# Fused attention and feed-forward layer: the two rounds of values and the round of ones of a four-step cycle are issued in one block

## The reference, cut to what matters

```python
# x: (2, 1024, 1024) f32; 32 heads of 32 channels, 8 key/value heads (4 heads share one)
xn = layernorm(x)
q, k, v = bitnet_linear(xn, wq, sq), bitnet_linear(xn, wk, sk), bitnet_linear(xn, wv, sv)
scores = einsum('bhqd,bhkd->bhqk', q, k) / sqrt(32)
out = einsum('bhqk,bhkd->bhqd', softmax(scores), v)
x + bitnet_linear(out, wo, so) + ffn(xn)      # ffn: silu(xn @ gate) * (xn @ up) @ down, 4-bit weights
```

## Time and profile before

| | |
|---|---|
| median of 3 runs | 2541.43 us (2540.97 to 2541.54) |
| the profiled execution | 2542.98 us, of which the span of the trace is 2541.0 us |
| mean granted TensorE clock, profiled execution | 0.967 of full speed |
| attention with its cycles in steady order (372 to 1151 us) | PE busy 777.61 of 779.00 us, DVE 608.92, ACT 609.37, POOL 710.12 |
| rest of the attention, without row products (1151 to 1193 us) | PE busy 35.34 of 42.00 us, ACT 33.17 |

### The profile page before, as it was taken

One profiled execution on the slowest core, in us unless ns is written; L12 is line 12 of the kernel. 1 busy time (PEld: TensorE's weight loads), 2 busy tenths in 40 slices (PEclk: granted clock), 3 DMA queues, 4 the chain that ended last, 5 costly groups with the idle time before them and its releaser, 6 DMA issues.

```text
span 2541.0 us, 33630 instructions
## 1 busy us (share of the span) xinstructions
PE 2384.1 (94%) x12408; PEld 969.4 (38%) x12408; DVE 1826.3 (72%) x2362; ACT 1549.7 (61%) x1988; POOL 983.7 (39%) x545
## 2 busy tenths in 40 slices
PE   2399899999999999997699999999999999999998
PEld 1344323333333333332344444444444444444444
DVE  6756587777777777771646777777777777777777
ACT  3533347777777777776225666666665566666664
POOL 1000038989999999998000121121001111221000
PEclk9599979999999999998799999999999999999999
DMA  4100035555555555564221111112112311113111
GB/s 171 66 4 34 11 79 82 87 90 81 91 79 88 90 82 91 79 93 60 100 95 42 34 50 34 34 50 100 42 37 98 106 34 34 50 34 145 64 41 67
DMA packets 173710, 174.65 MB, mean 69 GB/s; under 512 B 87586, under 2 KB 119202, under 8 KB 173558
## 3 DMA queue, kind: packets, MB, share of 16 engines
q1 hardware_dynamic: 111286, 150.62, 18.9%
q0 software_dynamic: 62272, 22.03, 11.3%
HBM read 160.08 MB, written 65.45 MB: 89 GB/s over the span
## 4 chain that ended last, share of the span: by engine, by line
PE 90%; DVE 4%; DMA 1%; ACT 1%; issue 1%; SPq 1%; POOL 1%; DVEq 0%; ACTq 0%; POOLq 0%
PE ps L1309 30%; PE ps L1325 15%; PE ps L1212 10%; PE ps L1185 10%; PE ps L1201 8%; PE ps L1160 7%; PE ps L1224 4%; PE ps L1289 4%; DVE zone L934 1%; DVE zone L812 1%; POOL zone L504 1%; PE ps L1341 0%; DMA zone<-in_L_attn_o_weight_dram 0%; DVE zone L781 0%; DVE zone L782 0%
## 5 line engine op out<-in xcount | busy, mean ns | idle before, releaser
L1309 PE MATMUL ps<-xT,zone 128*128 128x512 f16 x3584 | 774.6, 379 | 3.6 <-DVE zone L1098 2.8
L934 DVE TENSOR_REDUCE zone<-ps 128x1 f32<-128x512 f32 x1024 | 637.5, 682 | 180.2 <-PE ps L1185 180.2
L657 ACT ACTIVATE zone<-ps,sm 128x512 f32<-128x512 f32 x1024 | 626.1, 690 | 183.1 <-PE ps L1201 181.3
L504 POOL TENSOR_TENSOR zone<-zone 128x1024 f32<-128x1024 f32 x256 | 633.4, 2582 | 114.4 <-PE ps L1224 73.3
L1075 DVE TENSOR_SCALAR ps<-ps,zone_c 128x1024 f32<-128x1024 f32 x392 | 506.8, 1293 | 161.2 <-PE ps L1309 159.2
L725 ACT ACTIVATE ps<-ps,zone_c 128x1024 f32<-128x1024 f32 x392 | 426.6, 1088 | 261.4 <-PE ps L1309 259.6
L1309 PEld LDWEIGHTS ps<-xT,zone 128*128 128x128 f16 x3584 | 350.2, 98 | 427.3 <-DVE zone L1098 4.2
L1185 PE MATMUL ps<-zone 96*128 96x512 f16 x1024 | 402.5, 395 | 11.2 <-DMA zone<-zone 10.5
L1201 PE MATMUL ps<-zone 98*128 98x512 f16 x1024 | 388.2, 382 | 4.0 <-ACT zone L657 4.0
L1325 PE MATMUL ps<-zone 128*128 128x512 f16 x1792 | 387.1, 379 | 0.0
L1086 DVE TENSOR_SCALAR ps<-ps,zone_c 128x1024 f32<-128x1024 f32 x216 | 279.2, 1293 | 93.1 <-PE ps L1325 92.9
(11 more groups left out here) (127 smaller groups left out, 1281.8 us busy)
## 6 DMA issues: line engine op xcount, KB each, us to landing
zone<-dequantised SPq DMA_DIRECT2D x84, 512.0 KB, 3.6
dequantised<-zero_points SPq DMA_DIRECT2D x84, 256.0 KB, 4.0
zone<-zone SPq DMA_DIRECT2D x384, 32.0 KB, 2.3
zone<-_attn_hidden_states_dram SPq DMA_DIRECT2D x16, 512.0 KB, 6.5
zone<-inverse_sums SPq DMA_DIRECT2D x128, 64.0 KB, 2.1
attention<-zone SPq DMA_DIRECT2D x32, 256.0 KB, 2.0
xT<-attention SPq DMA_DIRECT2D x4, 2048.0 KB, 13.2
dequantised<-in_L_ffn_gate_w_dram POOLq DMA_DIRECT2D x28, 256.0 KB, 6.2
```

The lines of the kernel that those rows point to most:

```text
L504: nc.gpsimd.tensor_tensor(duo[n % 3], prob[:, e % 8, :], prob[:, (e + 2) % 8, :], add).then_inc(s["sum_ok"], 1)
L657: A(prob[:, e % 8, m % 2 * 512:(m % 2 + 1) * 512], ps[:, 3 + m % 3, :], ACT.Exp, scale=gam[:, 0:1]).then_inc(s["exp_ok"], 1)
L934: V.tensor_reduce(mxs[:, u % 2, half, i % 16:i % 16 + 1], ps[:, (2 * i + half) % 3, :], AX, amax).then_inc(s["max_ok"], 1)
L1309: last = MM(ps[:, 4 * s2 + 2 * m + c, :], ring[:, buf, m * H + g * P:m * H + (g + 1) * P], xT[:, hf, part, g, c * 512:(c + 1) * 512], star ...
```

## The change

The round of values with even kt leaves the steps with e % 4 == 2 and goes to the steps with e % 4 == 0, two steps later, directly ahead of the round of values with odd kt and the round of ones. After the loop the last even round (kt = 6 of unit 31) is issued with kt = 7. No instruction is added or removed, and no wait is changed.

```diff
                 if 2 * e + 4 < 2 * STEPS:
                     key_scores(2 * e + 4)
-                if e % 4 == 2:
-                    values(u, k // 2 - 1)
-                elif e % 4 == 0 and e >= 4:
+                if e % 4 == 0 and e >= 4:
                     t = e - 4
+                    values(t // 16, t % 16 // 2)
                     values(t // 16, t % 16 // 2 + 1)
                     if e >= 8:
                         pair_sums((e - 8) // 16, (e - 8) % 16 // 4)
                 elif k == 7 and u + 1 < UNITS:
                     maxima_rows(u + 1)
+            values(UNITS - 1, 6)
             values(UNITS - 1, 7)
             pair_sums(UNITS - 1, 2)
             pair_sums(UNITS - 1, 3)
```

## The result

The changed kernel takes 2611.19 us (median of 4 runs, 2608.89 to 2613.01), the kernel before 2541.48 us beside it (2540.97 to 2542.12). The ratio is 1.0274 with an interval of 1.0256 to 1.0291: slower by 2.7%, 70 us, where 2605 us was forecast.

The account below looks back on a forecast made before the run. PE was taken to bound the attention. Waits on banks add 58.8 us over 120 cycles, 3.9 in five last cycles and 0.8 in a half one: +63.5 us, 2605 us, range 2562 to 2625 (forecast's own 2592 to 2618).

Parts of the forecast that it names:

- PE bounds the attention: Steady attention: the chain of waits runs through PE alone, busy 777.61 of 779.00 us.
- A block of three rounds takes 3.01 us, and the saving is 0.25 us a cycle: Four-step cycle on PE: two values rounds and one ones round together; 6.30 us instead of 6.55 if nothing waits.
- Three banks make the eighth product wait for the fifth reader: Score bursts: last key product starts 3.79 us after the first row product, or 4.17, 4.17, 4.22 with ACT's other work.
- A unit of 28.39 us: Four cycles with row products: 28.39 us against 26.43, +1.96 us a unit, +58.8 us over 30 units.
- the half one at the end: The cycle with half its row products, after 120 full ones: +0.8 us.
- The last cycles, +3.9 us: Five cycles without row products at the attention's end: 34.4 us instead of 30.55.
- POOL is not reached: POOL's second addition of a cycle ends at 2.60 us, the first exponential needing it starts at 3.53: no cost.
- 1 (the readers keep up): Attention cycles: DVE and ACT keep pace, the 0.25 us a cycle is gained, -34 us, 2507 us; chance 0.05.
- 2 (ACT's other work hidden): Attention cycles: only the 3.79 us counts, all cycles near 6.80 us, 2567 us; chance 0.08.
- 4 (the addition comes late): Sixth key product's exponential waits for POOL by up to 0.5 us a cycle: up to +15 us, 2620 us; chance 0.06.
- 3 (the clock falls): PE in cycles with row products: one cycle in eight at 1.2 GHz, +83 us, 2688 us; chance 0.04.

Follow-up runs that it names:

- short readers: Maxima and exponentials read 256 of 512 columns, half left out: on the changed kernel 2519.14 us (0.9910), on the kernel before 2538.99 us (0.9986).
- experiments with one reader: The changed kernel with only the maxima, or only the exponentials, cut to 256 of 512 columns: 2602.97 us and 2579.04 us.
- maxima short: The changed kernel with the maxima alone reading 256 of 512 columns: 2602.97 us, ratio 1.0238 to the kernel before.
- short exponentials: The changed kernel with the exponentials alone reading 256 of 512 columns: 2579.04 us, ratio 1.0144 to the kernel before.

## Why the prediction was right

- *PE bounds the attention, and an idle microsecond on it is lost.* Right: short readers gave the kernel before only 4 us, while the changed kernel's waits on the banks made its unit 2.09 us longer, the saving taken off.
- *A block of three rounds takes 3.01 us, and the saving is 0.25 us a cycle.* Right: 3.02 us in the trace of the changed kernel, and 6.31 us for a cycle whose readers keep up. Only with short readers does the saving reach the result.
- *Three banks make the eighth product wait for the fifth reader: 3.79 us, or 4.17, 4.17 and 4.22 with ACT's other work.* In the trace it is 4.19 (605.12 to 609.31), 4.19 and 4.22 in the cycles with other work, and 3.79 (626.83 to 630.62) in the one without. In the chain L657 and L934 have 10.5% together, where some 8% was forecast. The experiments with one reader show who sets which: DVE the cycle without other work, ACT the three others.
- *A unit of 28.39 us.* It was 28.52, so 0.13 too small. The block takes 3.02 to 3.04, and two of the products that waited stand 0.02 later. The sum had 58.8 us for 120 cycles and 0.8 for the half one at the end. Measured between the first round of ones and the end of the row products, 119 cycles and the half one, are (1217.52 - 362.53) - (1155.32 - 362.54) = 62.2 us.
- *The last cycles, +3.9 us.* They took 1253.29 - 1217.52 = 35.77 us against 30.55: +5.2, of which 1.2 are a fall of the clock, told below. Another 2.5 us of span came behind them, which the sum had at nothing; what made these is not shown. With the 2.6 us of the stretch above they make the 6 us between 2605 and 2611.
- *POOL is not reached.* Right: its second addition starts 0.25 us after the block is left (605.12 to 605.37), and no wait of ACT for POOL shows in the steady part.

```profile
605.37 2.35 POOL L504 TENSOR_TENSOR zone<-zone 128x1024 f32<-128x1024 f32 x1 [1.03 <-PE ps L1224]
```

The rivals: 1 (the readers keep up) is refuted for this kernel and is what the short readers make of it. 2 (ACT's other work hidden) is refuted by the cycle lengths; moving two of the three pieces gained some 25 us. 4 (the addition comes late) did not occur. 3 (the clock falls) occurred once, for 3.4 us, and not in the cycles with row products for which it was priced.

## What to carry to other kernels

- A saving on the bounding engine that comes from putting like work together lengthens the bursts on both sides of it. Count the products in a burst against the buffers: the n-th waits for the reader of the one that stands as many places back as there are buffers, and from there the burst runs at the reader's step. Here 4 over 3 banks was free, 6 cost 0.2 us, 8 cost 0.5 us, and 0.9 us with other work in the reader's queue; the mean load of the readers, 78%, says nothing of it. Only three banks were run; for another number the rule is an extrapolation.
- An in-order reader's other work belongs in the time in which the producer gives it nothing. Moving two copies by one and two steps gained some 25 us in one order and 0.17% in the other, without one instruction more or less.

## What the runs showed beyond that

The clock fell once in the changed kernel's attention, in its last cycles, where only key products are left and PE waits in each. Stretches before, in and after it (length, busy time and count by engine, PEclk, DMA share, GB/s):

```profile
1215.00:1250.90 35.90, 28.17 (x170) 7.16 (x173) 0.90 (x4) 26.99 (x47) 31.50 (x18) 1.00 0.41 54
1250.90:1254.30 3.40, 3.40 (x24) 0.71 (x16) 0.00 (x0) 0.84 (x2) 0.91 (x1) 0.50 0.56 70
1254.30:1261.00 6.70, 4.23 (x35) 0.79 (x27) 0.00 (x0) 2.44 (x4) 5.96 (x4) 1.00 0.00 0
```

PE had been busy for 28.17 of 35.90 us (78%) when it went to 1.2 GHz for 3.4 us. Two rounds of values that take 1.92 us elsewhere took 3.16 there:

```profile
1243.34 1.92 PE L1212 MATMUL ps<-zone 128*32 128x512 f32 x16
...
1250.38 3.16 PE L1212 MATMUL ps<-zone 128*32 128x512 f32 x16
```

That is 1.2 us, most of what the last cycles lost over the forecast. In the steady part the clock stayed at its upper level, with PE busy for 819.09 of 843 us:

```profile
372.00:1215.00 843.00, 819.09 (x4755) 243.98 (x4753) 598.82 (x1065) 604.31 (x1036) 712.29 (x373) 1.00 0.52 79
```

The other traces narrow this down. In their last cycles the clock fell, for 3.4 us each time, twice with the maxima short (1227.1 and 1244.2 us) and once with ACT's work moved (1212.3 us), all in the changed order with full exponentials. While key products were being issued it did not fall in the two traces with short exponentials, nor in the four with shorter bursts. So it goes with the waits of key products for ACT in bursts of eight, though each kernel has only one trace, and what in these waits lets the clock fall is not shown. The rule weighed in rival 3 (the Trainium skill, TensorE: Matmul & The Clock Gate, "A second HAM failure mode: psum-queue depth-cycling") speaks of a clock that swings between its levels. This case agrees with it only in these single falls: 843 us with waits on the banks in every cycle show none.

With both readers short, ACT waited for POOL's additions, 25 times and 8.1 us in all, in the changed kernel:

```profile
ACT zone L657 <- POOL zone L504: 8.1, 25, 0.5
```

None of that shows in the cycle lengths above; of the waits between engines it is the one that comes closest next.
